# Cross attention with 257 keys: two chunks of 128 keys and a 257th key mixed in by VectorE, in place of three chunks of 86

## The reference, cut to what matters

```python
def _L1_xattn_ref(q, k, v, attn_mask, key_padding_mask, Wq, Wk, Wv, Wo):
    ...
    qh = (q @ Wq.T).reshape(B, Tq, H, hd).transpose(0, 2, 1, 3)
    kh = (k @ Wk.T).reshape(B, Tk, H, hd).transpose(0, 2, 1, 3)
    vh = (v @ Wv.T).reshape(B, Tk, H, hd).transpose(0, 2, 1, 3)
    ...
    scores = jnp.einsum('bhqd,bhkd->bhqk', qh, kh) / np.sqrt(hd)
    scores = scores + attn_mask
    scores = jnp.where(key_padding_mask[:, None, None, :], NEG_INF, scores)
    attn = jax.nn.softmax(scores, axis=-1)
    out = jnp.einsum('bhqk,bhkd->bhqd', attn, vh)
    out = out.transpose(0, 2, 1, 3).reshape(B, Tq, H * hd)
    return out @ Wo.T
...
    x = x + _L1_xattn_ref(_layernorm(x, axis=-1), ctx_1024, ctx_1024, mask_1x1xSxS2_fk0, mask_BxS2_bk0, L1_xattn_Wq, L1_xattn_Wk, L1_xattn_Wv, L1_xattn_Wo)
```

## Time and profile before

| | before |
|---|---|
| median of 3 runs | 2471.78 us (2469.35 to 2474.32) |
| the profiled execution | 2464.36 us, of which the span shown in the profile is 2462.7 us |
| PE busy over the span | 91% |
| DVE, ACT, POOL busy | 64%, 54%, 41% |
| cross attention, first to last `scores` | 1143.8 us to 1802.1 us of the span |

### The profile page before, as it was taken

One profiled execution on the slowest core, in us unless ns is written; L12 is line 12 of the kernel. 1 busy time (PEld: TensorE's weight loads), 2 busy tenths in 40 slices (PEclk: granted clock), 3 DMA queues, 4 the chain that ended last, 5 costly groups with the idle time before them and its releaser, 6 DMA issues. The chain is left out here.

```text
span 2462.7 us, 90206 instructions
## 1 busy us (share of the span) xinstructions
PE 2248.3 (91%) x32612; PEld 1707.5 (69%) x32613; DVE 1585.3 (64%) x4583; ACT 1336.3 (54%) x3729; POOL 1020.0 (41%) x924
## 2 busy tenths in 40 slices
PE   5989999987999879997999999999979999979994
PEld 3657777764888757775777777777756656666892
DVE  4567777764877543335777777777756766654442
ACT  3555555556777443333777777777755555542331
POOL 0023333322777400003555555555516666634115
PEclk9999999997999669998999999999989999989997
DMA  5630000000000000000111110111131000000112
GB/s 139 174 123 2 0 0 0 0 1 1 0 0 0 0 1 1 0 0 25 35 33 32 32 32 32 32 32 32 52 127 35 0 0 0 0 1 32 41 43 73
DMA packets 38094, 71.62 MB, mean 29 GB/s; under 512 B 6128, under 2 KB 26480, under 8 KB 37360
## 3 DMA queue, kind: packets, MB, share of 16 engines
q1 hardware_dynamic: 34672, 63.55, 8.5%
q0 software_dynamic: 3328, 6.82, 0.9%
HBM read 60.91 MB, written 9.44 MB: 29 GB/s over the span
## 5 line engine op out<-in xcount | busy, mean ns | idle before, releaser
L2297 DVE CUSTOM_DVE_ANT_0 xat_scores<-bank,xat_mask_b 128x257 f32<-128x257 f32 x512 | 212.5, 423 | 96.8 <-PE bank L2016 90.5
L2169 ACT ACTIVATE xat_scores<-xat_scores,xat_least 128x257 f32<-128x257 f32 x512 | 257.4, 503 | 12.1 <-DVE xat_least L2297 12.1
L2073 PE MATMUL bank<-ident,xat_scores 128*86 128x128 f32 x1536 | 240.4, 280 | 0.0
L2073 PEld LDWEIGHTS bank<-ident,xat_scores 128*86 128x86 f32 x1536 | 157.7, 122 | 83.5 <-ACT xat_scores L2169 40.9
L982 POOL TENSOR_TENSOR gqa_rnorm<-gqa_norm_min,gqa_minus_half 128x12 f32<-128x12 f32 x64 | 145.9, 2279 | 103.7 <-DVE gqa_norm_min L1059 103.7
L2183 ACT ACTIVATE xat_p_T<-bank 86x384 f32<-86x384 f32 x256 | 122.7, 480 | 121.8 <-PE bank L2073 121.8
L629 POOL TENSOR_TENSOR lin_q_softmax<-lin_q_exp,lin_q_rsum 128x512 f32<-128x512 f32 x64 | 66.8, 1043 | 246.0 <-DVE lin_q_rsum L685 246.0
L1599 DVE SCALAR_TENSOR_TENSOR X<-bank,expert_shares,X 128x128 f32 (+1 forms) x256 | 72.0, 343 | 149.0 <-PE bank L1564 149.0
L1585 ACT ACTIVATE moe_gelu<-bank 128x512 f32<-128x512 f32 x128 | 76.5, 597 | 145.7 <-PE bank L1556 145.7
L1323 POOL TENSOR_TENSOR bat_scores<-bat_scores,bat_max 128x512 f32<-128x512 f32 x128 | 131.9, 1041 | 55.8 <-DVE bat_max L1355 54.1
L1564 PEld LDWEIGHTS bank<-moe_w,moe_gelu 128*128 128x128 f32 x1024 | 124.2, 192 | 30.1 <-issue 18.7
(11 more groups left out here) (295 smaller groups left out, 5989.0 us busy)
## 6 DMA issues: line engine op xcount, KB each, us to landing
glu_ctx_N<-in_ctxN SPq DMA_DIRECT2D x32, 576.0 KB, 4.4
xat_ctx_T<-in_ctxT SPq DMA_DIRECT2D x32, 516.0 KB, 3.5
xat_pad<-in_xat_pad SPq DMA_DIRECT2D x32, 128.5 KB, 3.3
expert_w<-in_glx_w SPq DMA_DIRECT2D x1, 4096.0 KB, 14.4
slot_rows<-gqa_zero_rows SPq DMA_DIRECT2D x1, 2560.0 KB, 11.4
slt_rows<-slot_rows SPq DMA_DIRECT2D x40, 64.0 KB, 1.8
slot_results<-slt_y POOLq DMA_DIRECT2D x40, 64.0 KB, 1.8
moe_w<-in_moe_w SPq DMA_DIRECT2D x2, 1024.0 KB, 5.9
```

What stands on the lines that cost most here:

```text
L2073: m = pe.transpose(dst[0:JC, c * P:(c + 1) * P], sx[j % 2][g][:, c * JC:(c + 1) * JC], k.ident[:, :])
L2169: act.activation(sx[j % 2][g][:, 0:J], sx[j % 2][g][:, 0:J], ACT.Exp, bias=mn[j % 2][g][:, 0:1], scale=-1.0, accum_out=sm[j % 2][:, g:g + ...
L2297: dve.tensor_tensor_reduce(sx[j % 2][g][:, 0:J], pS[g][:, 0:J], mb[slot][:, j, :], 1.0, BIG, ALU.add, ALU.min, mn[j % 2][g][:, 0:1]).then_ ...
```

## The change

The keys are cut in NC = 2 chunks of 128, and the 257th key (`LAST`) is treated by itself. Its values for the four batches of a tile are one matmul `LC` (once per tile, with `v` of j = 0), copied by ACT to `v_last`. Its probabilities are spread over the features by four more matmuls (`PC`) in `v`, with 32 columns of weights each. DVE adds their product to the result of `o` in a new instruction, `o_mix`, before the normalising `o_keep`. `o_keep` reads SBUF alone now, and stands behind least 3. `nb` and the new `om` have two buffers. The zero column and its eight memsets go. POOL's `keep_mask` is split in two functions that are called one after the other.

```diff
-        va = [sb(f"v{i}", [JC, NJ, P]) for i in range(2)]
-        sx = [[sb(f"scores{i}_{g}", [P, JP]) for g in range(G)] for i in range(2)]
+        va = [sb(f"v{i}", [P, NC + 1, P]) for i in range(2)]
+        vl = [sb(f"v_last{i}", [P, BT]) for i in range(2)]
+        sx = [[sb(f"scores{i}_{g}", [P, J]) for g in range(G)] for i in range(2)]
...
-                for c in range(NJ):
+                for c in range(NC):
                     for g in range(G):
                         r = slice(32 * g, 32 * g + 32)
                         m = pe.matmul(dst[r, OC], va[j % 2][:, c, r], pt[j % 2][g][:, c * P:(c + 1) * P],
-                                      start=(c == 0), stop=(c == NJ - 1))
+                                      start=(c == 0), stop=(c == NC - 1))
                 m.then_inc(no_made, 1)
 
             def v(t, slot, j, at):
                 dst = unit_bank(*at)
-                for c in range(NJ):
-                    m = pe.matmul(dst[0:JC, c * P:(c + 1) * P], cT[slot][:, j, c * JC:(c + 1) * JC], wv[:, :],
-                                  start=True, stop=True)
+                if j == 0:
+                    pe.matmul(dst[:, LC], wv[:, :], cT[slot][:, :, LAST], start=True, stop=True)
+                for c in range(NC):
+                    pe.matmul(dst[:, c * P:(c + 1) * P], cT[slot][:, j, c * P:(c + 1) * P], wv[:, :],
+                              start=True, stop=True)
+                for g in range(G):
+                    m = pe.matmul(dst[32 * g:32 * g + 32, PC], sx[j % 2][g][:, LAST:J].broadcast_to([P, 32]),
+                                  k.ident[:, :], start=True, stop=True)
                 m.then_inc(v_made, 1)
...
-                for c in range(NJ):
-                    m = pe.transpose(dst[0:JC, c * P:(c + 1) * P], sx[j % 2][g][:, c * JC:(c + 1) * JC], k.ident[:, :])
+                for c in range(NC):
+                    m = pe.transpose(dst[:, c * P:(c + 1) * P], sx[j % 2][g][:, c * P:(c + 1) * P], k.ident[:, :])
                 m.then_inc(t_made, 1)
...
                 wait(act, no_made, u - 1)
-                act.activation(va[j % 2][:, :, :], unit_bank(*at)[0:JC, 0:NJ * P].rearrange("p (c f) -> p c f", f=P),
+                wait(act, o_mixed, u - 1)
+                if j == 0:
+                    act.activation(vl[slot][:, :], unit_bank(*at)[:, LC], ACT.Copy).then_inc(vl_copied, 1)
+                act.activation(va[j % 2][:, :, :], unit_bank(*at)[:, 0:PC.stop].rearrange("p (c f) -> p c f", f=P),
                                ACT.Copy).then_inc(v_copied, 1)
...
-                wait(dve, t_made, n - 2 * G + 1)
+                wait(dve, v_made, u - 1)
                 dve.sem_inc(dve_waited, 1)
...
-            def o_keep(t, slot, j, at):
-                dve.wait_ge(n_copied, BT * t + j + 1)
+            def o_mix(t, slot, j, at):
+                u = BT * t + j
+                dve.wait_ge(n_copied, u + 1)
+                dve.wait_ge(vl_copied, t + 1)
+                wait(dve, o_kept, u - 1)
+                dve.scalar_tensor_tensor(out=om[j % 2][:, :, :], in0=va[j % 2][:, NC, :].rearrange("p (h q) -> p h q", q=S),
+                                         scalar=vl[slot][:, j:j + 1],
+                                         in1=unit_bank(*at)[:, OC].rearrange("p (h q) -> p h q", q=S),
+                                         op0=ALU.mult, op1=ALU.add).then_inc(o_mixed, 1)
+
+            def o_keep(t, slot, j):
+                u = BT * t + j
+                dve.wait_ge(o_mixed, u + 1)
                 wait(dve, y_made, t - 1)
-                dve.tensor_tensor(os_[slot][:, :, j, :], unit_bank(*at)[:, OC].rearrange("p (h q) -> p h q", q=S),
-                                  nb[:, :, :], ALU.mult).then_inc(o_kept, 1)
+                dve.tensor_tensor(os_[slot][:, :, j, :], om[j % 2][:, :, :], nb[j % 2][:, :, :],
+                                  ALU.mult).then_inc(o_kept, 1)
...
                     least(t, slot, j, 2)
                     if more:
-                        o_keep(*two, (j, NO))
+                        o_mix(*two, (j, NO))
                     least(t, slot, j, 3)
+                    if more:
+                        o_keep(*two)
                     if some:
                         t_copy(*one, 3, (j, T3))
                         reciprocal(*one)
```

More of the change, by code:

```diff
@@ L1954, in stage_cross_attention @@
         rs = [sb(f"p_rsum{i}", [P, G]) for i in range(2)]
-        pt = [[sb(f"p_T{i}_{g}", [JC, NJ * P]) for g in range(G)] for i in range(2)]
-        nb = sb("rsum_of_row", [P, QH, S])
+        pt = [[sb(f"p_T{i}_{g}", [P, NC * P]) for g in range(G)] for i in range(2)]
+        nb = [sb(f"rsum_of_row{i}", [P, QH, S]) for i in range(2)]
+        om = [sb(f"o_mixed{i}", [P, QH, S]) for i in range(2)]
         os_ = [sb(f"o{i}", [P, QH, BT, S]) for i in range(2)]
@@ L2092, in body @@
                         if j == 1:
-                            wait(pe, o_kept, u - 2)
+                            wait(pe, o_mixed, u - 2)
                         else:
@@ L2122, in body @@
                     if j == 1 and not last:
-                        wait(pe, o_kept, u - 1)
+                        wait(pe, o_mixed, u - 1)
                         x_transpose(t + 1, 1 - slot, (j, XX))
                     if j == 2 and not last:
-                        wait(pe, o_kept, u - 1)
+                        wait(pe, o_mixed, u - 1)
                         q(t + 1, 1 - slot, (j, XX))
                     if j == 3 and not first:
-                        pe.wait_ge(o_kept, u - 1)
+                        pe.wait_ge(o_mixed, u - 1)
                         y(t - 1, 1 - slot, (j, XX))
@@ L2174, in n_copy @@
                 act.wait_ge(no_made, u + 1)
-                wait(act, o_kept, u)
-                act.activation(nb[:, :, :], unit_bank(*at)[:, RC].rearrange("p (h q) -> p h q", q=S),
+                wait(act, o_kept, u - 1)
+                act.activation(nb[j % 2][:, :, :], unit_bank(*at)[:, RC].rearrange("p (h q) -> p h q", q=S),
                                ACT.Copy).then_inc(n_copied, 1)
@@ L2182, in t_copy @@
                 wait(act, no_made, u - 1)
-                act.activation(pt[j % 2][g][:, :], unit_bank(*at)[0:JC, 0:NJ * P], ACT.Copy).then_inc(pa_copied, 1)
+                act.activation(pt[j % 2][g][:, :], unit_bank(*at)[:, 0:NC * P], ACT.Copy).then_inc(pa_copied, 1)
             def body(t, slot, first, last):
@@ L2364, in body @@
                     t_copy(t, slot, 3, 2, (0, T2))
-                    o_keep(t, slot, 2, (0, NO))
+                    o_mix(t, slot, 2, (0, NO))
+                    o_keep(t, slot, 2)
                     t_copy(t, slot, 3, 3, (0, T3))
                     reciprocal(t, slot, 3)
-                    o_keep(t, slot, 3, (0, XX))
+                    o_mix(t, slot, 3, (0, XX))
+                    o_keep(t, slot, 3)
                     add(t, (1, T1))
```

15 lines of the change are left out of this document (8 added, 7 removed).

## The result

The changed kernel takes 2453.54 us (median of 7 runs, 2448.23 to 2460.42), the kernel before 2469.35 on the same chip (7 runs, 2466.17 to 2474.32). The ratio is 0.9933, with a 95% interval of 0.9917 to 0.9949: 16.5 us are saved (13 to 20), where 39 were forecast. The direction is right and the time lies in the range, but more than half of the gain is missing.

A forecast was written before the change was run, and what follows sets the result against it. PE bounds two of four units, a chain ending on DVE the others. Units 4.45 + 4.74 + 4.91 + 5.36 = 19.46 against 20.73 us, 1.27 less per tile, 39 over 31 tiles: 2433 us, range 2416 to 2459.

The forecast's parts named there:

- A pass, 0.11, also at 128 keys: On PE: each matmul pass costs 0.11 us, and going from 86 to 128 keys in a chunk is free per pass.
- v's wait for DVE's copy, 0.10: On PE: v stands about 0.10 us for DVE's copy of T2 in all four units, with 0 to 0.2 possible.
- The gap ahead of `PC`: On PE: changing shape into the 32-column matmuls takes 0.20 us in place of an ordinary step of 0.11.
- The change back: On PE: returning from 32-column to full matmuls costs about 0.04 us behind the change, besides 0.09 ahead.
- DVE's durations: On DVE: copy of 256 columns 0.42 us, `o_mix` 0.34; the chain of steps to the next scores sums to 4.40.
- the forecast 4.45: Unit j = 0: DVE's chain of 4.40 us, over PE's 4.34, plus 0.05 for the loop's branch.
- `LC`, 0.20: On PE in j = 1: two passes with 128-column weights and four moving columns cost 0.20 us, bounds 0 and 0.22.
- j = 1, 4.88 for 4.74: Unit j = 1 on PE: 4.34 us plus 0.20 for x_transpose with its changes and 0.20 for `LC`, 4.74.
- Edits at no cost: On DVE: o_keep, 0.29 us or less, is hidden behind least 3 by a 0.68 us wait for scores.
- The forecast's own sign of being wrong: If units j = 2 and j = 3 do not fall about 0.3 us each, passes or changes of shape are dearer.
- the first rival: DVE's chain and v's wait take most of the gain: all units lose 0.2 us, time 2457, chance 0.21.

## Why the prediction was right and wrong

- **A pass, 0.11, also at 128 keys: right.** T3 starts 3.11 into the unit j = 3 (1450.01 - 1446.90), forecast 3.10.
- **v's wait for DVE's copy, 0.10: right, a little smaller.** The copy of T2 ends at 1450.20 and v's first load starts 0.05 behind it, in this unit as in the units j = 0 and j = 2. Before the change that load started 0.27 behind the copy, right behind the last transpose. The wait makes v's second pass come 0.18 behind the first and not 0.11, so it costs 0.07; in j = 1 `LC`'s load waits in v's place.

```profile
1449.78 0.42 DVE L2316 COPY xat_p_T<-bank 128x256 f32<-128x256 f32 x1
```

```profile
1450.25 0.52 PEld L2054 LDWEIGHTS bank<-xat_w_v,xat_ctx_T 128*128 128x128 f32 x4
```

- **The gap ahead of `PC`: right.** `PC` starts 4.00 into the unit and `y` 4.35 (1450.90 and 1451.25); the steps of the forecast, with the wait of v, give 3.99 and 4.34.
- **The change back, costed at 0.04: too small.** From `y` to the next scores are 1.09 (1451.25 to 1452.34), forecast 0.20 + 0.15 + 0.66 = 1.01. `y`'s eight passes last 1.16 behind `PC`, and 1.06 before; so it is 0.10 behind `PC`. These 0.10 are not the change of shape's own: `y` lasts 1.16 as well in the kernel without `PC`, where it stands behind a wait. From `x_transpose` to scores are 0.26 (1461.44 to 1461.70), forecast 0.20. These 0.06 to 0.08 fall on three units, and are j = 3's whole miss (5.44 for 5.36).
- **DVE's durations: right; its steps, by luck.** The copy has a mean of 414 ns (forecast 0.42), `o_mix` 348 (0.34), ACT's copy of 256 columns 376 (0.38). least 0 starts 1.35 into j = 1 where 1.42 was taken, and least 1 follows after 0.35 (0.39). But k_cos comes 0.51 behind least 1 and not 0.36 (1458.56 and 1459.07), and the copy starts 2.89 into the unit, forecast 2.85: errors that cancel. j = 0 at 4.43 is the forecast 4.45.
- **`LC`, 0.20: right**, with 0.21. It does not go by at once.
- **j = 1, 4.88 for 4.74.** With the operand in PSUM it is 4.83, so 0.05 is `o_keep`'s stop; 0.06 is the change back, and the last 0.03 are not placed.
- **"Edits at no cost: o_keep (0.29 or less) now runs behind least 3": this step failed.** The cover was there, and the place is worth its 0.43. But the duration came from a row in which the instruction had an operand in PSUM. With both in SBUF it lasts 0.877 in the mean and up to 2.18. DVE's slack ahead of j = 2 covers an `o_keep` of 1.09 and not one of 2, and the copy of T3 is then late for PE. I had said what the cover would cost if it were gone (0.29 in each unit; it is 0.43 in j = 0 and nothing in the others), and not asked whether the instruction could become longer than the cover.
- **The forecast's own sign of being wrong came, and the reason that it gave for it did not.** j = 2 and j = 3 were to fall by about 0.3 each. j = 3 fell by 0.21 (5.65 to 5.44), for which the dearer start of `y` is the reason. j = 2 grew by 0.35 (5.19 to 5.54), and neither passes nor changes of shape did that.

The books of a tile: 20.30 measured against 19.46 forecast. j = 2 has 0.63 of the 0.84 (0.57 from the stop, 5.54 against 4.97; 0.06 from the change back), j = 1 0.14, j = 3 0.08, j = 0 -0.02. The stop takes 0.64 of a tile in all (20.30 against 19.66), 20 us in 31 tiles. The size thus landed at the first rival's 2457, and an instruction on DVE was indeed what took the gain. But the mechanism was another: not all four units lost 0.2 each; one lost 0.57. That the time lies near this rival's, and in the range, is luck.

No row under the prediction shows such a stop: no instruction of DVE in the units shown there read two SBUF tensors. The operand lists of the change could have warned, and so could the trace of the kernel before, at one place. Ahead of the first `scores` DVE multiplies two SBUF tensors of 1028 columns once, and POOL's product runs beside it. In the kernel before DVE came second, by 0.19 us, and took 3.19 us:

```profile
1137.95 3.19 DVE L2333 TENSOR_TENSOR xat_mask_kept<-xat_keep,xat_mask_negated 128x1028 f32<-128x1028 f32 x1
```

```profile
1137.76 2.30 POOL L2227 TENSOR_TENSOR xat_ctx_kept<-xat_keep,xat_ctx_T 128x1028 f32<-128x1028 f32 x1 [0.28 <-DMA xat_ctx_T<-in_ctxT]
```

In the profile of the change DVE came first there, by 0.05 us. It took 1.23, and now POOL's product took 3.21, where it takes 2.19 alone:

```profile
1140.79 1.23 DVE L2356 TENSOR_TENSOR xat_mask_kept<-xat_keep,xat_mask_negated 128x1028 f32<-128x1028 f32 x1 [0.94 <-POOL xat_keep L2265]
```

```profile
1140.84 3.21 POOL L2241 TENSOR_TENSOR xat_ctx_kept<-xat_keep,xat_ctx_T 128x1028 f32<-128x1028 f32 x1
```

## What to carry to other kernels

When an edit moves an operand from PSUM to SBUF, cost the instruction anew: if it now reads two tensors from SBUF on DVE, look at what POOL does at that moment, and take POOL's longest instruction as the bound, not the mean. A stall of this kind is known by its end, which lies a fixed step behind the end of the other engine's instruction whatever its start; it is cured by an operand in PSUM, or by cutting the other engine's long instruction into pieces that are shorter than the slack. And a term set at zero for its cover needs both numbers, the cover and the longest that the covered thing can take.

## What the runs showed of the hardware

- A product of two SBUF tensors (128 x 128, f32) on DVE took 285 ns with POOL idle and up to 2179 ns beside POOL's 2.19 us product; its end was 0.14 to 0.16 us behind POOL's in all 88 cases of the changed kernel's profile. With one operand in PSUM it took 286 ns beside the same POOL work.
- Which instruction of POOL it was did not matter: the product (L2241), the sum (L2247) and the conversion from `uint8` (L2230, which ended at 1451.61; `o_keep`, begun at 1451.10, ended at 1451.75) stopped it. In these cases POOL's product kept its 2.19 us. Whichever came second stood: at the start of the stage DVE's product of 1028 columns took 3.19 us behind POOL's and 1.23 ahead of it, where POOL's took 3.21.
- A matmul with 128 weight columns and only four moving ones, two passes, costs 0.21 us on PE, no less than full ones.
- A train of full matmuls in two passes that starts behind a pause costs 0.10 more in its first step: `y` lasts 1.16 behind the 32-column matmuls and 1.16 behind a wait, and 1.06 without a pause. Back to transposes it is 0.04.
- The rest of the program varies between profiles and chips (the kernel before took 2466.52 to 2503.60 in the medians of four comparisons), while the stage repeated within 0.8 us; so the lengths of units in the stage say more on a single term than the totals.
